# A selective-scan block with modulation and routed experts: sixteen small copies of a gate table are issued by SyncE instead of GpSimd

## What is computed

```python
x = L0_attn_u                                     # (8, 1024, 256)
mod = (_silu(L0_c) @ L0_wmod).reshape(8, 6, 1, -1)
sa, ca, ga, sb, cb, gb = (mod[:, i] for i in range(6))
ga = (2 * (ga >= 0) - 1) * jnp.maximum(jnp.abs(ga), 0.25)
gb = (2 * (gb >= 0) - 1) * jnp.maximum(jnp.abs(gb), 0.25)
h = _layernorm(x) * (1 + ca) + sa
# scan: dt = softplus(..), h_t = exp(dt*A) h_(t-1) + (dt*u) B,  y = sum_n C_n h_n + u*D
x = x + ga * selective_scan(h, ...)
h = _layernorm(x) * (1 + cb) + sb
x = x + gb * top2_of_8_experts(h, ...)
```

## Time and profile before

| | us |
|---|---|
| median of 3 runs | 1194.52 |
| the three runs | 1186.55, 1194.52, 1194.61 |
| the profiled execution | 1194.61 |
| its span (first to last instruction) | 1192.8 |

### The profile page before, as it was taken

One profiled execution on the slowest core, in us unless ns is written; L12 is line 12 of the kernel. 1 busy time (PEld: TensorE's weight loads), 2 busy tenths in 40 slices (PEclk: granted clock), 3 DMA queues, 4 the chain that ended last, 5 costly groups with the idle time before them and its releaser, 6 DMA issues. The chain is left out here.

```text
span 1192.8 us, 13296 instructions
## 1 busy us (share of the span) xinstructions
PE 935.6 (78%) x4235; PEld 594.6 (50%) x4235; DVE 1007.0 (84%) x794; ACT 701.9 (59%) x1331; POOL 932.1 (78%) x322
## 2 busy tenths in 40 slices
PE   6345444599977898789977997788879997889898
PEld 5111112256654555455644665455645665556787
DVE  2499999898999999999999999999989898995210
ACT  4854578546874589557865688458855366331200
POOL 3376666599887999699969998798969988698463
PEclk9656665688989999999999999998989898889999
DMA  6607050634335461737245443547163533521221
GB/s 201 143 18 194 18 123 0 152 124 127 104 75 146 125 169 36 179 106 173 66 117 168 118 122 71 141 127 175 38 151 99 139 91 85 136 73 45 86 76 62
DMA packets 90294, 131.19 MB, mean 110 GB/s; under 512 B 13280, under 2 KB 73256, under 8 KB 90224
## 3 DMA queue, kind: packets, MB, share of 16 engines
q1 hardware_dynamic: 89712, 130.31, 42.0%
q0 software_dynamic: 512, 0.03, 0.0%
HBM read 54.50 MB, written 8.65 MB: 53 GB/s over the span
## 5 line engine op out<-in xcount | busy, mean ns | idle before, releaser
L972 POOL TENSOR_TENSOR h<-h,Cr 128x2048 f32<-128x2048 f32 x129 | 581.1, 4505 | 164.2 <-DVE h L849 128.7
L849 DVE TENSOR_TENSOR_SCAN h<-av,ps 128x1024 f32<-128x1024 f32 x256 | 585.1, 2286 | 24.8 <-ACT av L639 5.7
L596 PE MATMUL ps<-xg,we 128*128 128x256 f32 x2048 | 503.1, 403 | 4.4 <-POOL xg L1010 4.2
L596 PEld LDWEIGHTS ps<-xg,we 128*128 128x128 f32 x2048 | 404.5, 202 | 105.2 <-issue 39.0
L1010 POOL TENSOR_TENSOR xg<-h2T,gbc 128x1024 f32<-128x1024 f32 x128 | 303.1, 2371 | 65.7 <-PE ps L596 27.9
L842 DVE TENSOR_TENSOR ps<-ps,dd 128x1024 f32<-128x1024 f32 x256 | 315.4, 1232 | 34.5 <-PE ps L481 12.2
L639 ACT ACTIVATE av<-dd,An 128x1024 f32<-128x1024 f32 x256 | 290.0, 1141 | 87.0 <-DVE h L849 75.5
L500 PE MATMUL ps<-h,gam 128*32 128x512 f32 x1024 | 154.5, 731 | 31.3 <-POOL h L972 28.3
L481 PE MATMUL ps<-S,sel 64*128 64x512 f32 x128 | 52.8, 496 | 67.9 <-DVE ps L842 67.7
L727 ACT ACTIVATE z<-ps,md 128x256 f32<-128x256 f32 x64 | 26.7, 468 | 101.6 <-PE ps L604 86.6
L500 PEld LDWEIGHTS ps<-h,gam 128*32 128x32 f32 x1024 | 30.6, 126 | 107.7 <-issue 70.8
(11 more groups left out here) (100 smaller groups left out, 744.3 us busy)
## 6 DMA issues: line engine op xcount, KB each, us to landing
dd<-src SPq DMA_DIRECT2D x512, 128.0 KB, 2.4
gbc<-gates SPq DMA_DIRECT2D x128, 256.0 KB, 3.6
X<-in_x SPq DMA_DIRECT2D x8, 1024.0 KB, 10.0
out<-X SPq DMA_DIRECT2D x32, 256.0 KB, 3.5
XN<-in_x SPq DMA_DIRECT2D x7, 1024.0 KB, 7.7
we<-in_We SPq DMA_DIRECT2D x2, 1024.0 KB, 8.9
XN<-in_x SPq DMA_DIRECT2D x2, 512.0 KB, 4.4
Cr<-in_wmod SPq DMA_DIRECT2D x1, 1024.0 KB, 5.6
```

What stands on the lines that cost most here:

```text
L596: e = pe.matmul(bk[:, m * 256:(m + 1) * 256], we[:, hf, 2 * ep + e2, m * P:(m + 1) * P], xg[:, i % XG, e2, hf], start=(ep == e2 == m == hf ...
L849: dve.tensor_tensor_scan(h[:, u % HS], av[:, u % AS], wide(BP), 0.0, ALU.mult, ALU.add).then_inc(s_scan, 1)
L972: pool.tensor_tensor(hu, hu, Cr[:, q:q + 1].to_broadcast([P, n, L]), ALU.mult).then_inc(s_ch, n)
```

## The change

The 16 copies of `ga` leave POOL's stream and are issued by SP. Their due time in the table goes from -40.0 to -0.84, which sets where they stand in SP's stream. The copies themselves, their semaphore and the wait for `s_md` stay as they are.

```diff
-          gates=-31.95, ga=-40.0, bn0=-124.93, ...
+          gates=-31.95, ga=-0.84, bn0=-124.93, ...
@@ sync engine, in its walk over the plan
+                elif s[0] == "ga":
+                    sp.wait_ge(s_md, 2)
+                    for nl in range(4):
+                        for j in range(NJ):
+                            sp.dma_start(ga4[32 * nl:32 * nl + 32, j], md[32 * j:32 * j + 32, 4:6]).then_inc(s_ga, 16)
@@ GpSimd, in its walk over the plan
-                elif s[0] == "ga":
-                    pool.wait_ge(s_md, 2)
-                    for nl in range(4):
-                        for j in range(NJ):
-                            pool.dma_start(ga4[32 * nl:32 * nl + 32, j], md[32 * j:32 * j + 32, 4:6]).then_inc(s_ga, 16)
```

More of the change, by code:

```diff
@@ L31 @@
           gw=11.28, gr=27.35, xg=23.26, xgs=1.78, gl=-2.22, f=-3.09, fE=0.44, o=2.08, oX=1.54, out=12.44, md1=-53.75,
-          gates=-31.95, ga=-40.0, bn0=-124.93, bn0s=14.46, stat1A=5.1, stat1B=8.15, stat1sA=-6.79, stat1sB=2.89,
+          gates=-31.95, ga=-0.84, bn0=-124.93, bn0s=14.46, stat1A=5.1, stat1B=8.15, stat1sA=-6.79, stat1sB=2.89,
           rstd1A=5.94, rstd1B=7.94, rsb1A=0.8, rsb1B=5.29, xh1A=6.94, xh1B=44.04, xh1sA=0.05, xh1sB=0.52, xh1gA=32.69,
```

## The result

| | before | after |
|---|---|---|
| median of 20 runs, us | 1190.0 | 1197.82 |
| lowest and highest | 1186.55, 1195.48 | 1193.28, 1199.95 |
| span of the profiled execution | 1192.8 | 1197.1 |

The ratio is 1.0054, with a 95% interval of 1.0042 to 1.0067: the changed kernel is 6.4 us (5.0 to 8.0) slower, within the 1% that was called no change, and inside the predicted range. Twenty runs of the kernel before have a median of 1190.0, 4.5 us under that of the first three, from which the prediction started. One run of the kernel before, of 1822.8 us among the later experiments, was slow and stands in no ratio.

The account below looks back on a forecast made before the run. DVE's unbroken row of scans from 56 us on was taken as the bound, so only its start counts. 0 for POOL, 2.2 for ACT's late start and 0 for copies to dd, on 1194.61, gave 1196.8 us, range 1187.5 to 1202.5.

Parts of the forecast that it names:

- The bound and the rigid shift: From 56 us on DVE sets the pace, so a later start of its scans moves everything behind equally, 2.2 us.
- a sign that it is wrong: After 60 us, the distance between the two kernels' scans growing or shrinking would show the prediction wrong.
- POOL's issues give nothing back: On POOL before gam, the 16 issues of 8.01 us go away, but gam waits for ga's landing anyway: 0.
- SP's rate: On SP from 22.98 us, 16 ga issues at 0.60 us each take 9.6 us, so batch 1's load leaves at 32.58.
- The load's landing: Batch 1's load lands 6.2 us after issue, at 38.78; ACT waits 3.1 us before the first decay.
- The cover of 0.9 us: DVE's old waits for dd at the third and fourth multiplies, 0.89 us, absorb part of ACT's 3.1, leaving 2.2.
- gam and the queue to dd: gam delays later dd copies 1.1 us; queued first copies land 2.5 us late, shrinking; cost at the fourth multiply 0.
- A load nearly hidden: Rival: SP issues at 0.50 us, the load lands at 36.9, ACT waits 1.2 us; +0.3, 1194.9 us; chance 0.20.
- The queue behind the load: Rival: dd copies stay 2.5 us late, plus 1.1 for gam; fourth multiply 3.6 us late, 1198.2 us; chance 0.15.
- Slow issues of over 1.2 us: Rival: small issues slow on SP, at 1.54 us each ACT waits 18.1 us; +17.2, 1211.8 us; chance 0.07.
- a gain: Rival: SP's ga copies land sooner, the load still in time, SP's 0.24 us pause goes; 1194.4 us; chance 0.05.

Follow-up runs that it names:

- The changed kernel's second profile: The changed kernel timed and profiled once more beside the kernel before, on another chip; nothing else changed; median 1197.55 us, ratio 1.0020.
- the late load alone: Against the kernel before, with ga still issued by POOL: SP issues batch 1's load only after all 16 ga copies landed; median 1195.62 us, ratio 1.0026.
- ga behind the load: Against the changed kernel: due time of ga 1.0 instead of -0.84, so SP issues batch 1's load, then ga, then dd; median 1193.33 us, ratio 1.0025.
- the shorter pad: Against the kernel before: a fill and three idle multiplies on DVE ahead of the fifth multiply; median 1200.11 us, ratio 1.0064.
- The longer pad: Against the kernel before: a fill and six idle multiplies on DVE ahead of the fifth multiply; median 1201.10 us, ratio 1.0064.

## Why the prediction was right

**The bound and the rigid shift: right only between profiles with the same clock.** The row of scans started late, and the changed kernel's profile ends 4.3 us later for 3.85 us at the mark, but in between the distance shrinks to nothing and grows to 5.8. The prediction named that as a sign that it is wrong, and in the pair of the result the sign is there. What varies is the length of a batch: the third takes 134.6 us in the kernel before and 130.3 in the changed kernel (from the load at 249.64 or 253.96 to the next), at a mean clock of PE of 0.90 and 0.92 between 250 and 384 us, where DVE's waits for PE add up to 4.0 and 1.4 us. DVE is then not the only thing that sets the pace, and the prediction had no term for this. The changed kernel's second profile, with the clock of the kernel before, keeps its distance (4.5 to 4.9).

**POOL's issues give nothing back: right.** 7.7 us of its busy time are gone from the page, and no step comes sooner for it.

**SP's rate: right.** 0.63 us per issue, where 0.60 was taken and 0.62 was the bound from dd. The load went out at 32.65 (32.58 forecast). POOL's own rate of 0.50 was no guide. One issue is short beside its copy's 1.7 us to land; it is the 16 in a row, 10.08 us, that hold up what stands behind them.

**The load's landing: right in kind, too small.** This is the term of the sum that was mis-sized. 6.2 us was taken, from a place where copies to dd had just gone ahead. Here they came behind, and it took 7.5 (7.9 in the second profile of the changed kernel, 7.0 with the late load alone, 5.6 with ga behind the load, where nothing followed for ten microseconds but small copies). With ACT ready at 35.41 (40.21 - 4.80), the wait was 4.8 instead of 3.1 us.

**The cover of 0.9 us: nearly.** Between the first scan and the fourth multiply 10.39 us passed before and 9.71 after, so 0.7 us were taken up. Put together from one profile each, the first scan is 4.53 us late and 0.7 is absorbed: 3.85 instead of the forecast 2.2. Of the 1.65 us missing, the larger part is the term for the landing. With the scatter of the marks (63.62 and 64.29 after, 59.6 to 60.3 before) the start costs some 4 us, so the forecast had a little over half of it.

**gam and the queue to dd lie beside it: right.** Forecast were 1.1 us for gam and nothing left of the queue's 2.5 us at the fourth multiply. Measured were 0.8 (37.00 against 36.23) for the second four copies, and landings of 6.6 us falling to 2.6. With ACT's wait out of the way these effects cost 1.5 us at the mark, less than the 3.85 beside which they lie. The queue shrank by 0.2 us per us (4.0 over the 19 us from 33.4 to 52.3), faster than the 0.12 that was read from a later stage.

**Where the time came from.** The runs explain 3.85 to 4.1 us of the 6.4. In the 20 runs each that were timed first, the lower groups lie at 1189.5 (11 runs, median) and 1193.3 (one run, whose mean clock of 0.874 makes its place uncertain), the upper at 1193.8 (nine) and 1197.9 (nineteen): 3.8 and 4.1 us apart. The rest, some 2.4 us, is the mix: 11 of 20 runs in the lower group before, 1 of 20 after. With another mix on another chip the whole difference was 2.4 us (ratio 1.0020). That the moved copies cause a worse mix is not shown, nor that the later start does; it stays open. The prediction had the 8 us between its first three runs as unexplained, and its starting point of 1194.5 was in the upper group; that its 1196.8 comes so near to 1197.8 is in good part luck, as the loss was put at 2.2 us and measured at 6.4.

**The rivals.** A load nearly hidden (+0.3) would have needed SP to issue at POOL's rate. The queue behind the load (+3.6) has almost the right size at the mark and is the wrong cause: the fourth multiply of the changed kernel waits for no copy, and with ACT's wait gone only 1.5 us remain. Slow issues of over 1.2 us do not occur for ga, and a gain had nothing to come from.

## What to carry to other kernels

Sixteen issues on a queue with nothing behind them gave back nothing when they left it; the same issues put ahead of others in a busy queue cost some 4 us here. One has to list what waits behind them, the next batch's load as well as the copies at hand. The engine that pays may be a third one: here ACT, whose statistics for a later batch stood ahead of the first decay. And where two chains end together, taking time off one buys almost nothing (4.3 us off the first scan, at most 0.6 at the mark), while adding to either costs most of what is added: 3.7 us at the first scan gave 3.0 at the mark, and 3.9 us in SP's queue gave 5.0.

## What the runs showed that was not expected

**A load lands later with copies right behind it.** The load of batch 1, 1 MB, landed after 5.6 to 6.0 us in the six profiles in which no copy to dd followed for 8 us or more, and after 7.0 to 7.9 in the four in which full copies followed within 0.7 to 1.8 us. In the kernel with ga behind the load 64-byte rows followed at once, and it landed after 5.6: many small followers did not slow it. That the followers are the cause is argued, as no run moved them alone. In the three profiles in which SP had just issued ga, the issue of the load itself took 0.58 us instead of 0.37, which is a part of their 7.5 to 7.9 beside the 7.0 of the late load alone.

**A DVE multiply beside POOL's.** The pads came out longer than planned. By tile, in the shorter pad, the idle multiplies (min, median and max in ns), and from POOL's timeline what ran beside them:

```profile
L927 DVE TENSOR_TENSOR xg<-xg x3: 1224/1224/4620, 61.3 to 67.2; 128x1024 f32<-128x1024 f32 x3
```

```profile
60.33 4.51 POOL L977 TENSOR_TENSOR h<-h,Cr 128x2048 f32<-128x2048 f32 x1 [3.11 <-DVE h L849]
```

Two of the three take 1.22 us; the first, from 61.3 on, takes 4.62, while POOL multiplies from 60.33 to 64.84. The longer pad shows the same once in six (4.62 us), while POOL multiplies from 59.66 to 64.18. Both times DVE's multiply ends 1.1 us behind POOL's, as if it had hardly begun before (the profile's spans on POOL are rough). DVE's usual multiply reads one operand from the matrix engine's banks and takes 1.23 us, also beside POOL (from 63.62 in the changed kernel, say, where POOL multiplies from 63.65). One placement in each of two kernels shows it; its cause was not tried.

**Two groups of runs, and the clock.** From the mark to the end the profiles take 1126.6 to 1127.2 us or 1131.1 to 1138.2. What goes with it is PE's granted clock, here as the mean of a stretch (1.0 is its upper level of 2.4 GHz, 0.5 its lower of 1.2 GHz). In the two profiles with 1127.2 it is 0.95 from 250 to 774 us. In those with 1131.1 and more it is 0.90 to 0.92 in the stretch from 250 to 384 us and, in five of the seven, at 0.91 or less from 384 to 514 as well. The same stretch, 384 to 514 us, in the changed kernel and in the one with the late load alone (third column from the end: the clock):

```profile
384.00:514.00 130.00, 112.43 (x518) 71.74 (x516) 122.41 (x91) 88.02 (x172) 113.18 (x35) 0.91 0.47 120
```

```profile
384.00:514.00 130.00, 110.46 (x525) 70.41 (x524) 124.36 (x92) 89.01 (x173) 115.09 (x36) 0.95 0.48 123
```

At 0.91 a batch takes 131.6 us in the one (from its load at 384.22 to the next at 515.84), at 0.95 it takes 129.6 in the other (381.48 to 511.10), though DVE, not PE, is the busiest engine in both. The longer pad, with 1126.6, has 0.91 too, but in another place (514 to 644 us, a batch of 133.3 us), and 0.95 from 774 to 906, where the others have 0.91 or 0.92. So each profile has batches that are 2 to 5 us longer at a lower clock, and how many and which they are makes the groups. Which of the two is cause and which is effect, these profiles do not tell.
